# Order of the small steps in an attention pipeline: inversion behind the masks, output copies and scaling later

## The reference

```python
qkv = jnp.einsum('bsm,qhdm->bqhsd', x, W_qkv)          # 16 heads of 64
qk_rot = qk * cos + _rotate_half(qk) * sin             # first 32 dims of q and k
scores = jnp.where(causal, -jnp.inf, einsum('bhqd,bhkd->bhqk', Q, K)) / sqrt(64)
out = einsum('bhqk,bhkd->bhqd', softmax(scores), V)    # then projected by W_o
...
top_v, top_i = jax.lax.top_k(softmax(x @ router_w + router_b), 2)   # 8 experts and a skip
h = gelu(einsum('btd,edf->ebtf', x, w1)); y = einsum('ebtf,efd->ebtd', h, w2)
```

## Time and profile before

| | us |
|---|---|
| median of 3 runs | 1500.76 (1494.09 to 1503.2) |
| profiled execution | 1500.74 |
| its span | 1499.0 |
| PE busy | 1254.0 (84%) |
| DVE busy | 1195.7 (80%) |
| ACT busy | 1122.6 (75%) |
| POOL busy | 858.6 (57%) |

### The profile page before, as it was taken

How to read it: one execution, slowest core, us unless ns; L and a number is a source line. 1 busy time by engine, 2 the same in 40 slices (tenths; PEclk the granted TensorE clock), 3 DMA queues, 4 the chain that set the end, 5 groups by cost and what they waited for, 6 DMA issues and landing times.

```text
span 1499.0 us, 46446 instructions
## 1 busy us (share of the span) xinstructions
PE 1254.0 (84%) x15156; PEld 940.5 (63%) x15157; DVE 1195.7 (80%) x4018; ACT 1122.6 (75%) x3606; POOL 858.6 (57%) x1194
## 2 busy tenths in 40 slices
PE   1416999888888898895999999888888889888888
PEld 1404666666666666664889898566666666666666
DVE  5788877777777887783777777889988889889886
ACT  6415888877787787784878887878777777777786
POOL 3254777777777777773000000767777777666775
PEclk9757999999999999997999999999999999999999
DMA  9621433333333333333232322333333333333330
GB/s 290 204 56 38 101 73 73 74 72 72 74 72 74 72 80 79 75 83 111 72 88 84 87 84 75 77 80 79 80 82 92 91 84 80 89 91 89 85 80 27
DMA packets 115831, 130.12 MB, mean 87 GB/s; under 512 B 11568, under 2 KB 75312, under 8 KB 115376
## 3 DMA queue, kind: packets, MB, share of 16 engines
q1 hardware_dynamic: 107056, 110.26, 30.6%
q0 software_dynamic: 8576, 17.33, 3.8%
HBM read 28.85 MB, written 31.59 MB: 40 GB/s over the span
## 4 chain that ended last, share of the span: by engine, by line
PE 28%; DVE 22%; DMA 17%; POOL 16%; issue 13%; ACT 4%; POOLq 0%; DVEq 0%; SPq 0%; ACTq 0%
DMA sorted_x_dram<-stage,slots 17%; PE bank L1102 6%; PE bank L1103 6%; PE bank L1104 6%; DVE arena L956 4%; POOL sorted_x_dram L497 3%; POOL arena L476 3%; PE bank L1173 3%; DVE arena L919 2%; DVE arena L918 2%; POOL arena L456 2%; PE bank L1184 2%; POOL arena L457 2%; ACT probs L643 2%; PE bank L1211 2%
## 5 line engine op out<-in xcount | busy, mean ns | idle before, releaser
L643 ACT ACTIVATE probs<-arena,neg_max 128x128 f32<-128x128 f32 (+1 forms) x1024 | 452.3, 446 | 110.5 <-DVE neg_max L956 108.5
L956 DVE CUSTOM_DVE_ANT_0 arena<-bank,causal 128x128 f32<-128x128 f32 (+1 forms) x1024 | 302.3, 349 | 46.6 <-PE bank L1173 46.1
L507 POOL DMA_INDIRECT stage<-sorted_y_dram,slots x128 | 130.5, 1020 | 257.9 <-DVE arena L919 238.6
L1184 PE MATMUL bank<-ident,probs 128*128 128x128 f32 x1536 | 212.6, 275 | 13.5 <-ACT probsT L626 10.7
L633 ACT ACTIVATE o_whole<-bank 128x256 f32<-128x256 f32 x256 | 97.7, 382 | 151.5 <-PE bank L1195 85.2
L497 POOL DMA_INDIRECT sorted_x_dram<-stage,slots x128 | 133.3, 1041 | 128.6 <-DMA sorted_x_dram<-stage,slots 104.2
L1184 PEld LDWEIGHTS bank<-ident,probs 128*128 128x128 f32 x1536 | 177.2, 142 | 39.6 <-issue 18.4
L643 ACT ACTIVATION_READ_ACCUMULATOR probs<-arena,neg_max 128x1 f32 x1024 | 194.7, 190 | 0.0
L1102 PE MATMUL bank<-arena 128*128 (+1 forms) x864 | 183.2, 238 | 1.5 <-DVE arena L1076 1.5
L476 POOL TENSOR_TENSOR arena<-o_whole,arena 128x256 f16<-128x256 f32 x256 | 172.0, 672 | 21.0
L1103 PE MATMUL bank<-arena 128*128 (+1 forms) x864 | 182.7, 238 | 0.0
(11 more groups left out here) (152 smaller groups left out, 3258.8 us busy)
## 6 DMA issues: line engine op xcount, KB each, us to landing
arena<-arena SPq DMA_DIRECT2D x256, 256.0 KB, 3.8
arena<-sorted_x_dram SPq DMA_DIRECT2D x72, 128.0 KB, 2.2
sorted_y_dram<-stage SPq DMA_DIRECT2D x72, 128.0 KB, 1.8
sorted_x_dram<-arena SPq DMA_DIRECT2D x3, 2304.0 KB, 17.8
arena<-experts_dram SPq DMA_DIRECT2D x8, 512.0 KB, 5.6
out_dram<-acc SPq DMA_DIRECT2D x32, 128.0 KB
sorted_x_dram<-arena SPq DMA_DIRECT2D x1, 2368.0 KB, 19.1
sorted_x_dram<-stage,slots POOLq DMA_INDIRECT x128, 2.5
```

The costliest lines, as they stand in the source:

```text
L643: last = nc.scalar.activation(probs[:, s % 4, at:at + w], masked[:, s % 4, at:at + w], ACT.Exp, bias=neg_max[:, s % 4, t:t + 1], scale=-1. ...
L956: last = nc.vector.tensor_tensor_reduce(out=masked[:, (s + i) % 4, at:at + w], in0=SC[i][:, at:at + w], in1=causal[:, at:at + w], scale=1. ...
L1184: last = nc.tensor.transpose(TP[s % 2][:, k * P:(k + 1) * P], probs[:, s % 4, k * P:(k + 1) * P], ident[:])
```

## The change

Four moves. (1) PE makes the projection units of a period ahead of the turned inverse sums. (2) ACT copies the output behind the exponentials instead of ahead of them. (3) DVE scales the output one period later, ahead of the masks, and POOL splits it one period later (`SPLIT_LAG` 5). (4) DVE inverts directly behind the masks, ahead of the turn. The units of a period are also sorted otherwise: in p 5 rest 0 comes ahead of y 1, in p 7 rest 1 ahead of v_low 1.

```diff
-T_LAG, PV_LAG, OUT_LAG, INV_LAG, SPLIT_LAG, BACK_LAG = 1, 2, 2, 3, 4, 2
+T_LAG, PV_LAG, OUT_LAG, INV_LAG, SPLIT_LAG, BACK_LAG = 1, 2, 2, 3, 5, 2
@@ def plan(b):
-    steps = [(p, kind, j, b if kind == "v_high" else b - 1 if kind == "y" else b + 1)
-             for p, kind, j in (OPENERS if b in (0, MID) else USUAL) if nearer or kind in ("v_high", "y")]
-    steps += [(p, kind, j, b + 2) for p, kind, j in AHEAD if further]
+    opening = b in (0, MID)
+    steps = [(p, kind, j, b + 2) for p, kind, j in AHEAD if further]
+    steps += [(p, kind, j, b if kind == "v_high" else b - 1 if kind == "y" else b + 1)
+              for p, kind, j in (OPENERS if opening else USUAL) if nearer or kind in ("v_high", "y")]
     steps += [(p, kind, j, b + 1) for p, kind, j in VALUES if nearer]
-    return sorted(steps, key=lambda step: (step[0], step[1] == "rest" or step[0] == 6 and step[1] == "v_low"))
+    return sorted(steps, key=lambda step: step[0])
@@ ACT, sample
                     turned(past(b, p, OUT_LAG))
+                    for s in (2 * p, 2 * p + 1):
+                        exps(b, s, at == OPENING)
                     then = past(b, p, INV_LAG)
                     if then:
                         o_copy(8 * then[0] + then[1], then[1])
-                    for s in (2 * p, 2 * p + 1):
-                        exps(b, s, at == OPENING)
@@ DVE, sample
+                    then = past(b, p, INV_LAG + 1)
+                    if then:
+                        o_scale(8 * then[0] + then[1], then[1])
                     masks(b, 2 * p)
+                    then = past(b, p, 2)
+                    if then and p % 2 == 0:
+                        invert(4 * then[0] + then[1] // 2, then[1] // 2)
                     for kind, j, of, u, psum in units_at(b, p):
                         if kind == "rope":
                             turn(j, u, psum, of)
-                    then = past(b, p, INV_LAG)
-                    if then:
-                        o_scale(8 * then[0] + then[1], then[1])
-                    then = past(b, p, 2)
-                    if then and p % 2 == 0:
-                        invert(4 * then[0] + then[1] // 2, then[1] // 2)
@@ DVE, rest_of
+                o_scale(8 * b + 4, 4)
                 o_scale(8 * b + 5, 5)
@@ PE, sample
                     scores(b, 2 * p, parity, at == OPENING)
+                    for kind, j, of, u, psum in units_at(b, p):
+                        unit(kind, j, of, of % 2, psum, bank_free(u))
                     then = past(b, p, INV_LAG)
                     if then:
                         turn_sums(*then)
-                    for kind, j, of, u, psum in units_at(b, p):
-                        unit(kind, j, of, of % 2, psum, bank_free(u))
```

## The result

The changed kernel takes 1577.37 us, median of four runs (1574.78 to 1580.71), against 1497.42 for the kernel before (1493.47 to 1503.2, four runs beside it): a ratio of 1.0543 with a 95% interval of [1.0515, 1.0571]. The forecast of 1508 and its whole range of 1482 to 1531 were too low. The profiled execution took 1578.59 us, its span is 1576.9.

What follows compares the result with a forecast made beforehand. It took POOL's round with its sends to bound the first half, the round of DVE, ACT and PE the second. 1500.7 +12 (first half) -6 (second half) +1.5 (ends) = 1508 us, range 1482 to 1531.

Steps and rivals of the forecast that it cites:

- the one on y 0: First half, p 4: y 0 needs the last split, now behind one more send; PE sits longer, costed at nothing further.
- the slower rival: First half: PE stands in p 4 until the late split, with later work queued; 2 us per sample, 1532 us, chance 0.22.
- From the start of y 0 PE needs: Second half, PE: 2.92 us from the start of y 0 to the scores of p 5, without a pause.
- From the masks of p 2 to those of p 6: Second half: 16.60 us before, 16.7 forecast with y 0 taking over; net 0, bounds -0.6 and +0.6.
- Start of y 0 behind the masks of p 2: Second half: y 0 waits for the split and starts 8.6 us behind these masks.
- Masks of p 6 to 7: Second half: 4.36 us before; inversion ahead of the turn avoids POOL's rotation, 0.6 us off, to 3.8.
- p 7 to 0: Second half, between masks: 4.12 us before; output copy replaces value copy, scaling stands behind the wait; net +0.2 us.
- p 0 to 1: Second half, between masks: 5.90 us before, all DVE; earlier inversion gives -0.3 us, bounds -0.8 and +0.3.
- p 1 to 2: Second half, between masks: 3.93 us before; output copy ahead of ACT's high part adds 0.3 us.
- The sum of -0.4 us per sample: Second half, all terms between masks together: -0.4 us per sample, 15 samples, -6 us, bounds -22 and +10.
- the late masks: First half: p 7's copy needs that period's split, delaying p 0's masks and POOL's p 1 rotation; +0.8 us per sample.
- They are not the gain: Second half: PE's 41.7 us of waits for inverse sums end, but bank waits replace them; DVE work ends unchanged.

Runs made afterwards that it cites:

- run 1: The changed kernel with the split lag put back from five to four, all else as changed: 1509.31 us, 1.0012 to before.
- run 2: The kernel before with only the split lag raised from four to five: 1577.33 us, 1.0471 to before.
- run 4: The changed kernel with y 0 moved beside y 1 in p 5, both ahead of the period's other units: 1517.85 us, 1.0067 to before.
- Run 3: The changed kernel with useless filler matmuls on PE ahead of y 0 (20 in the first half, 8 in the second): 1539.13 us, 1.0194 to before.
- run 5: The changed kernel with the split lag back at four and y 0 beside y 1 in p 5, ahead of other units: 1518.42 us, 1.0152 to before.
- run 12: The changed kernel with the split lag back at four and the inversion back behind the turn: 1499.59 us, 1.0037 to before.
- run 7: The kernel before with only DVE's inversion moved directly behind the masks: 1479.51 us, 0.9895 to before.

## Why the prediction was wrong

**The step that failed first** is the one on y 0: "It now stands behind one more send ... I cost this at nothing beyond the above, because the other engines wait for POOL at that point anyway". The mechanism was seen and its cover was misjudged. ACT's 61.3 us of waits for POOL are a mean lead of 4 us in a sample, but PE's wait rose by 40.9 us, and what stood behind it, scores, exponentials, masks and turns, came late for POOL's rotation (41.7 us of waiting in the first half). POOL then sent later, and the loop was closed: lead can be spent once, a loop that is longer than the period is paid in every sample. This was the slower rival, with the right place and a price of 2 us per sample (1532 us); measured are 3.8. That POOL's late sends close the loop is read from these waits; runs 1, 2 and 4 show that the lag and y 0 are where the loss starts.

**The step that neither the forecast nor the rival had** is "From the start of y 0 PE needs 1237.13-1234.21 = 2.92 to the scores of p 5". That stretch was taken from the earlier trace rows as a fixed duration, and it is wrong twice. The turned sums, which move (1) puts behind y 0, are not in it: with them it takes 3.39 us at full clock. And behind a pause of 1.93 us it takes 4.9 in nine samples of thirteen, because TensorE runs at its lower clock. From the masks of p 2 to those of p 6 I had forecast 16.7 us; measured are 1275.39-1256.38 = 19.0 in a sample with a drop and 17.5 in one without. Of the 2.3 us too little 1.5 are the clock and 0.5 the turned sums. Run 3 shows the clock's part the other way round. The pause itself, forecast at "about 0.7 to 1 us or more", is 1.93.

**Second half, the other terms.** Start of y 0 behind the masks of p 2: 8.6 forecast, 8.7 measured. Masks of p 6 to 7: 3.8 and 3.97. p 7 to 0: 4.3 and 4.26. p 0 to 1: 5.6 and 5.58. p 1 to 2: 4.2 and 4.24. The inversion's last step, which was to come down "nearer 0.2 than 0.5", did so (kernel after, 1000 to 1550 us):

```profile
L973 DVE SCALAR_TENSOR_TENSOR inv_parts<-inv_total,inv_parts x61: 166/167/339, 1004.5 to 1545.6; 128x8 f16<-128x8 f32 x61
```

The sum of -0.4 us per sample was off by 1.6: 36.51-35.35 = 1.16. Held against the 35.5 us of most samples without a drop it is off by 0.55, nearly all of it the turned sums (0.47); the drops add 1.5 us in nine of 13 samples, 1.0 in the mean. The 16.60 us that I read for p 2 to 6 in the kernel before were also too few: the sample of the earlier trace rows is one of the short ones, 34.9 us to the next mix, and in the samples behind it the same distance is 17.1.

**First half, the late masks.** The path by ACT's copy of p 7 and POOL's split (+0.8 us) was not what decided: ACT waits 2.7 us in all for POOL, twice. With y 0 late the other engines come to p 7 behind POOL, so the split is there when they ask. Whether the term is real where y 0 is in time, no run parts: with y 0 out of the way the lag costs 37.0-35.67 = 1.3 us a sample (runs 4 and 5), more than the 0.8 forecast and by ways not traced here. In run 4 y 0 still waits 0.4 to 0.8 us for POOL in most first-half samples, so part of it is the gate.

**"They are not the gain".** I said of PE's waits for inverse sums that they end but win nothing, because other readings of banks would take their place. Beside the other moves that holds: run 1, with the inversion first, is not clearly faster than run 12 without it, and by its trace it is slower. Alone in before it does win: run 7 is 1.05% faster, 1.76 us per sample in the second half, where 41.7 us in 520 were waited. Only 0.4 of these lie between the masks of p 6 and 7 (3.94 against 4.36), where I had forecast 0.6. The forecast counted the shorter instruction there and nothing for the inverse that comes earlier.

**Where my range failed.** Its upper end took 2 us per sample for the rival, in the first half alone. It had nothing for a clock that depends on the pauses of PE. The steady sample of the earlier trace rows doesn't show this price: its longest pauses of PE are 1.10 and 1.24 us, and the clock there is 1.00. But the trace of before has it once, at the end of the first half, where y 0 waits for the same split. Timeline of PE, then window (columns as above):

```profile
699.41 0.22 PE L1102 MATMUL bank<-wvo_lo,arena 128*128 128x128 f16 x1 [2.30 <-POOL arena L476]
```

```profile
700.00:705.00 5.00, 3.88 (x41) 3.71 (x38) 1.27 (x3) 0.00 (x0) 0.00 (x0) 0.66 0.02 3
```

Behind a pause of 2.30 us the mean clock of five microseconds is 0.66. I did not ask what a new pause of this kind would do in each sample.

**What is open.** How the 3.8 us of the first half divide between the wait and the clock is only bounded: the filler wins 1.36 us of them back, y 0 a period later 2.2, and the stretch behind y 0 is 1.9 us longer than at full clock. Whether a drop needs the pause in a certain place is not known; in run 1's first half 12 of 14 samples have a pause of 1.3 to 2.1 us ahead of y 0, and the clock drops behind four of them (mean clock 0.98). A kernel with all four moves, a lag of five, y 0 later and PE's units back was not run, so whether the change can be made to pay is not known.

## What to carry to other kernels

A buffer's release that moves by one period moves behind everything its engine does in that period: look for the consumer that needs the last of the set (here y 0, which needs all eight splits) and give it the same period, or leave both. Look ahead of it too: here the split at its old place would have stood in the period of the scaling that it waits for. Don't take the duration of a TensorE stretch as fixed behind a new pause: add the price of half clock for it, and count what your own change moves into the stretch. An order in which PE waits in many short pieces, or where nobody is queued behind it, may avoid the price; that was not tried. A change of several moves is worth being tried move by move: here the inversion alone was the gain (-1.05%), copy and scaling together a loss beside a split lag of four (+1.6%), and one number cost 5%. The price of a move holds only beside the moves it was measured with: the inversion first wins 1.76 us a sample alone and loses 0.6 beside the others.

## What was not expected of the hardware

A pause of TensorE of 1.93 us in a stretch where it is 92% busy (459.18 of 500 us) can be enough for the granted clock to fall to 0.50 for some 3 us and cost 1.5 us of work, nearly as much as the pause itself; it fell in nine of 13 samples with equal pauses. Behind these short pauses the drop comes on the instructions that end them: in the sample shown the clock is 1.00 from 1264 to 1265 us, inside the pause, and 0.50 from 1266 on. In the pauses of over 4 us of the first half it can come earlier: from 648.0 to 649.2 us, just ahead of the y 0 at 649.29, it is already 0.50. And matmuls that nobody needs made the changed program 38 us faster.
